# Xattn and mixture-of-experts layer on one core: the first stage with loads in order of use, a query projection in two halves, and large GpSimd work put later

## The reference

```python
x = x + xattn(layernorm(x), ctx)      # x (8, 112, 512), ctx (8, 375, 128)
x = x + ffn(layernorm(x))

def xattn(q, latent_kv):              # 16 heads of 32
    qp = q @ Wq.T                     # (512, 512)
    k, v = split(latent_kv @ Wkv_expand.T, 2)
    scores = einsum('bhqd,bhkd->bhqk', qh, kh) / sqrt(32)
    attn = softmax(where(tril, scores, min))
    return (attn @ vh) @ Wout.T

def ffn(h):                           # 896 tokens, 8 experts, the best 2 of each token
    combine = top2(softmax(h @ gate.T))
    y = sum_e combine[e] * (silu(h @ gate_e.T) * (h @ up_e.T)) @ down_e.T
    return y + shared_expert(h)
```

## Time and profile before

| | |
|---|---|
| median of 3 runs | 365.05 us (364.71 to 365.6) |
| profiled execution | 365.72 us |
| its span, first to last instruction | 364.0 us |
| mean granted TensorE clock | 0.985 |
| busy, share of the span | PE 94%, PEld 77%, DVE 70%, ACT 64%, POOL 28% |
| instructions | 6,824 |

### The profile page before, as it was taken

One profiled execution on the slowest core, in us unless ns is written; L12 is line 12 of the kernel. 1 busy time (PEld: TensorE's weight loads), 2 busy tenths in 40 slices (PEclk: granted clock), 3 DMA queues, 4 the chain that ended last, 5 costly groups with the idle time before them and its releaser, 6 DMA issues.

```text
span 364.0 us, 6824 instructions
## 1 busy us (share of the span) xinstructions
PE 340.8 (94%) x2212; PEld 280.3 (77%) x2213; DVE 255.8 (70%) x460; ACT 231.5 (64%) x607; POOL 101.3 (28%) x111
## 2 busy tenths in 40 slices
PE   5599899999999998999999899999999999999992
PEld 5487778677777676898898788878888887888871
DVE  2994885899975518782676897787778778777810
ACT  3525888999976222512136488888887887888731
POOL 3649221455550000054600003112211311221131
PEclk9889999999999999999999999999999999999997
DMA  7999000000000859995779753543444354344333
GB/s 226 366 367 377 27 2 2 3 2 0 3 3 2 307 167 398 357 392 193 257 245 216 262 163 58 81 90 60 66 82 84 58 82 92 59 67 82 53 38 52
DMA packets 28458, 49.46 MB, mean 136 GB/s; under 512 B 6672, under 2 KB 11792, under 8 KB 27408
## 3 DMA queue, kind: packets, MB, share of 16 engines
q1 hardware_dynamic: 24288, 39.91, 33.6%
q0 software_dynamic: 4144, 9.23, 14.8%
HBM read 32.22 MB, written 16.92 MB: 135 GB/s over the span
## 4 chain that ended last, share of the span: by engine, by line
PE 71%; ACT 13%; DMA 6%; DVE 5%; issue 3%; POOLq 1%; POOL 0%; SPq 0%; DVEq 0%; ACTq 0%
PE bank L501 30%; PE bank L778 21%; ACT prob L900 9%; PE bank L793 9%; DMA out<-y_sb,dest 3%; PE bank L684 3%; PE bank L817 2%; DMA w_kv<-wkvT 2%; PE bank L656 2%; PE bank L493 1%; ACT probT L855 1%; DMA w_sg<-sguT 1%; DVE xn L1122 1%; PE bank L670 1%; PE bank L579 1%
## 5 line engine op out<-in xcount | busy, mean ns | idle before, releaser
L1129 DVE TENSOR_TENSOR gu_parts<-w_gu,gu_parts 128x704 fp32r<-128x704 f32 x84 | 72.8, 888 | 21.2 <-ACT gu_parts L855 19.7
L855 ACT ACTIVATE gu_parts<-w_gu 128x704 fp32r x84 | 66.1, 790 | 15.8 <-PE bank L778 15.4
L482 POOL DMA_INDIRECT out<-y_sb,dest x21 | 33.1, 1575 | 145.7 <-ACT y_sb L1050 137.7
L778 PE MATMUL bank<-gu_parts,xsT_hi 128*128 128x352 f32 x336 | 69.9, 330 | 1.2 <-issue 1.2
L778 PEld LDWEIGHTS bank<-gu_parts,xsT_hi 128*128 128x128 f32 x336 | 55.3, 189 | 2.2 <-issue 2.2
L778 PE MATMUL bank<-gu_parts,xsT_lo 128*128 128x352 f32 x168 | 40.8, 324 | 0.0
L793 PE MATMUL bank<-w_dn,actT_plain 128*128 (+1 forms) x80 | 37.7, 592 | 0.0
L501 PE MATMUL bank<-x2T_hi,w_sg_lo 128*128 128x512 f32 (+1 forms) x88 | 32.2, 365 | 0.1
L501 PE MATMUL bank<-x2T_hi,w_sg_hi 128*128 128x512 f32 (+1 forms) x88 | 31.9, 363 | 0.0
L501 PE MATMUL bank<-x2T_lo,w_sg_hi 128*128 128x512 f32 (+1 forms) x88 | 31.9, 363 | 0.0
L778 PEld LDWEIGHTS bank<-gu_parts,xsT_lo 128*128 128x128 f32 x168 | 29.3, 189 | 0.0
(11 more groups left out here) (199 smaller groups left out, 769.9 us busy)
## 6 DMA issues: line engine op xcount, KB each, us to landing
w_gu<-guT SPq DMA_DIRECT2D x8, 1408.0 KB
xs_dram<-xs_in SPq DMA_DIRECT2D x1, 5460.0 KB, 20.3
xs_in<-xs_dram SPq DMA_DIRECT2D x21, 256.0 KB, 2.7
w_dn<-dnT SPq DMA_DIRECT2D x8, 512.0 KB, 5.2
w_sg<-sguT SPq DMA_DIRECT2D x10, 256.0 KB
xres<-x SPq DMA_DIRECT2D x2, 768.0 KB, 9.6
w_dn<-dnT SPq DMA_DIRECT2D x8, 192.0 KB, 5.5
w_sd<-sdnT SPq DMA_DIRECT2D x5, 256.0 KB, 6.1
```

Source lines behind the costliest of these rows:

```text
L482: pool.indirect_dma_start(out=out[:, :], out_offset=bass.IndirectOffsetOnAxis(ap=dest[:, i, 0:1], axis=0), in_=y_sb[i % 2][:, :], in_offse ...
L778: ins = pe.matmul(dst[:, 0:F], xsT[x_][:, c, :], gu2[w_][:, c, f0:f0 + F], start=c == 0 and n == 0, stop=c == C - 1 and n == 2)
L855: act.activation(dst, src, ACT.Copy).then_inc(s[sem], 1)
L1129: dve.tensor_tensor(lo_, src, hi_.bitcast(F32), ALU.subtract).then_inc(s[sem], 1)
```

## The change

The loads are issued in another order and in smaller pieces: x tile 0, ctx 0, the key half of w_kv, x tile 1, x tiles 2 and 3, w_q in four chunks of 128 rows, the value half of w_kv, the remaining x tiles, ctx 1, w_o, then the shared weights. The keys are made before `t1(1)`. The query projection of the first four tiles is made in two halves: first 256 tokens (tiles 0 and 1) chunk by chunk, each chunk waiting only for its own split, with the transposes of tiles 2 and 3 between; then the other 256 tokens, block j by block j, with the transposes of tiles 4 to 6 behind blocks 1 to 3. GpSimd's subtractions of w_kv and w_q go to VectorE. GpSimd splits w_o in eight pieces after the seventh normalised tile, and fills the constants after attention block 1. The split of the first slices of the shared weights goes to attention block 1, on ScalarE before `put_oT(1)` and on VectorE before `oT_lo(1)`. In the diff below, the list of semaphore names and the body of the constants, which moved unchanged, are cut.

```diff
--- before.py
+++ after.py
@@ -227,11 +227,11 @@
...
@@ -258,13 +258,17 @@
                 at = slice(k * BLK, (k + 1) * BLK)
                 sp.dma_start(ctx[:, at, :], ctxT[:, at, 0:SQ]).then_inc(s[f"ctx{k}"], 16)
+            sp.dma_start(xres[:, 0, :], x_rows[0:P, :]).then_inc(s["x0"], 16)
             load_ctx(0)
-            sp.dma_start(xres[:, 0, :], x_rows[0:P, :]).then_inc(s["x0"], 16)
-            sp.dma_start(w_kv[:, :], wkvT).then_inc(s["wkv"], 16)
-            sp.dma_start(xres[:, 1:BLK, :], tiles_of(x_rows, 1, BLK)).then_inc(s["x0b"], 16)
-            sp.dma_start(w_q[:, :, :], wqT.rearrange("(c p) d -> p c d", p=P)).then_inc(s["wq"], 16)
+            sp.dma_start(w_kv[:, 0:H], wkvT[:, 0:H]).then_inc(s["wkeys"], 16)
+            sp.dma_start(xres[:, 1, :], x_rows[P:2 * P, :]).then_inc(s["xt1"], 16)
+            sp.dma_start(xres[:, 2:BLK, :], tiles_of(x_rows, 2, BLK)).then_inc(s["xt2"], 16)
+            for c in range(C):
+                sp.dma_start(w_q[:, c, :], wqT[c * P:(c + 1) * P, :]).then_inc(s[f"wq{c}"], 16)
+            sp.dma_start(w_kv[:, H:2 * H], wkvT[:, H:2 * H]).then_inc(s["wvals"], 16)
             sp.dma_start(xres[:, BLK:NX, :], tiles_of(x_rows, BLK, NX)).then_inc(s["xrest"], 16)
             load_ctx(1)
+            sp.dma_start(w_o[:, :, :], woT.rearrange("(c p) d -> p c d", p=P)).then_inc(s["wo"], 16)
             def load_sg(j):
@@ -280,7 +284,6 @@
             load_sg(0)
             load_sd(0)
-            sp.dma_start(w_o[:, :, :], woT.rearrange("(c p) d -> p c d", p=P)).then_inc(s["wo"], 16)
             sp.dma_start(w_gate[:, :, :], gateT).then_inc(s["wgate"], 16)
             load_sg(1)
             load_sd(1)
@@ -406,41 +409,35 @@
             rstd(0, "st1", var1, rstd1, mv1, "rs1a", "rs1b")
-            pool.wait_ge(s["wkv_hi"], 1)
-            pool.tensor_tensor(w_kv2[1][:, H:2 * H], w_kv[:, H:2 * H], w_kv2[0][:, H:2 * H].bitcast(F32), ALU.subtract)\
-                .then_inc(s["wkv_lo2"], 1)
-            for n in range(1, BLK):
+            for n in range(1, NX):
                 rstd(n, "st1", var1, rstd1, mv1, "rs1a", "rs1b")
-            pool.wait_ge(s["wq_hi"], 1)
-            half = slice(C // 2, C)
-            pool.tensor_tensor(w_q2[1][:, half, :], w_q[:, half, :], w_q2[0][:, half, :].bitcast(F32), ALU.subtract)\
-                .then_inc(s["wq_lo2"], 1)
-            for n in range(BLK, NX):
-                rstd(n, "st1", var1, rstd1, mv1, "rs1a", "rs1b")
+            pool.wait_ge(s["xn"], NX)
             pool.wait_ge(s["wo"], 16)
-            pool.tensor_copy(w_o2[0][:, :, :], w_o[:, :, :]).then_inc(s["wo_hi"], 1)
-            pool.wait_ge(s["wo_hi"], 1)
-            pool.tensor_tensor(w_o2[1][:, :, :], w_o[:, :, :], w_o2[0][:, :, :].bitcast(F32), ALU.subtract)\
-                .then_inc(s["wo_lo"], 1)
-            own(pool.memset(tri[:, :], 1.0))
...
-            pool.iota(token, [[P, NX], [0, 1]], base=0, channel_multiplier=1).then_inc(s["tok"], 1)
+            for c in range(C):
+                pool.tensor_copy(w_o2[0][:, c, :], w_o[:, c, :]).then_inc(s["wo_hi"], 1)
+            for c in range(C):
+                pool.wait_ge(s["wo_hi"], c + 1)
+                pool.tensor_tensor(w_o2[1][:, c, :], w_o[:, c, :], w_o2[0][:, c, :].bitcast(F32), ALU.subtract)\
+                    .then_inc(s["wo_lo"], 1)
+            def constants():
+                own(pool.memset(tri[:, :], 1.0))
...
+                pool.iota(token, [[P, NX], [0, 1]], base=0, channel_multiplier=1).then_inc(s["tok"], 1)
             def apply2(n):
                 pool.wait_ge(s["rs2b"], n + 1)
                 pool.tensor_scalar(x2n[:, n, 0:H], xres[:, n, :], mv2[:, n, 0:1], rstd2[:, n, :],
@@ -452,6 +449,8 @@
                     apply2(n - 3)
                 for r in range(RP, R):
                     normalised(n, r)
+                if n == 1:
+                    constants()
             for n in (NX - 2, NX - 1):
                 rstd(n, "st2", var2, rstd2, mv2, "rs2a", "rs2b")
@@ -513,6 +512,11 @@
             def q_proj(k, j, bank_):
                 product(bank_[:, 0:WX[k]], [(both(w_q2, every, c, slice(j * P, (j + 1) * P)), both(xnT[k], every, c, every))
                                         for c in range(C)]).then_inc(s["Q"], 1)
+            def q_part(c, j, cols, bank_):
+                return product(bank_[:, cols], [(both(w_q2, every, c, slice(j * P, (j + 1) * P)), both(xnT[0], every, c, cols))],
+                               start=c == 0, stop=c == C - 1)
             def k_proj(k, j, bank_):
                 product(bank_[:, 0:W], [(both(w_kv2, every, slice(j * P, (j + 1) * P)),
@@ -583,20 +587,34 @@
             t1(0, S[0])
             for what in ("ctx_hi", "ctx_lo", "wkv_hi", "wkv_lo"):
                 pe.wait_ge(s[what], 1)
-            k_proj(0, 0, bank[4])
-            for j in range(1, C):
+            for j in range(C):
                 k_proj(0, j, bank[4 + j])
-                t1(j, S[j])
-            pe.wait_ge(s["xnT_lo"], 2)
-            keep_busy(S[0:2], 5)
-            for what, value in (("wq_hi", 2), ("wq_lo", 1), ("wq_lo2", 1), ("xnT_hi", BLK), ("xnT_lo", BLK)):
-                pe.wait_ge(s[what], value)
+            t1(1, S[1])
+            keep_busy(S[2:4], 6)
+            first, second = slice(0, 2 * P), slice(2 * P, 4 * P)
+            for c in range(C):
+                pe.wait_ge(s["wq_hi"], c + 1)
+                pe.wait_ge(s["wq_lo"], c + 1)
+                if c == 0:
+                    pe.wait_ge(s["xnT_hi"], 2)
+                    pe.wait_ge(s["xnT_lo"], 2)
+                for j in range(C):
+                    if c == 0:
+                        pe.wait_ge(s["KT"], j + 1)
+                    q_part(c, j, first, bank[4 + j])
+                if c in (1, 2):
+                    t1(c + 1, S[c + 1])
+            pe.wait_ge(s["xnT_hi"], BLK)
+            pe.wait_ge(s["xnT_lo"], BLK)
             for j in range(C):
-                pe.wait_ge(s["KT"], j + 1)
-                q_proj(0, j, bank[4 + j])
-                if BLK + j < NX:
-                    t1(BLK + j, S[j])
-            pe.wait_ge(s["wkv_lo2"], 1)
+                for c in range(C):
+                    ins = q_part(c, j, second, bank[4 + j])
+                ins.then_inc(s["Q"], 1)
+                if j >= 1:
+                    t1(BLK + j - 1, S[j - 1])
+            pe.wait_ge(s["wkv_hi"], 2)
+            pe.wait_ge(s["wkv_lo"], 2)
             pe.wait_ge(s["QT"], C - 1)
             v_proj(0)
             pe.wait_ge(s["xnT_hi"], NX)
@@ -637,8 +655,8 @@
                         if b >= 3:
                             pe.wait_ge(s["x1"], b - 2)
                         if b == 2:
-                            pe.wait_ge(s["wo_hi"], 1)
-                            pe.wait_ge(s["wo_lo"], 1)
+                            pe.wait_ge(s["wo_hi"], C)
+                            pe.wait_ge(s["wo_lo"], C)
                         out_proj(b - 2, 0, 7)
                     if r == 1 and b >= 3:
                         t2(b - 3, CC)
@@ -917,26 +935,32 @@
                 hi(ctx2[0][:, at, :], ctx[:, at, :], "ctx_hi")
             ctx_hi(0)
-            act.wait_ge(s["wkv"], 16)
-            hi(w_kv2[0][:, :], w_kv[:, :], "wkv_hi")
+            def wkv_hi(sem, at):
+                act.wait_ge(s[sem], 16)
+                hi(w_kv2[0][:, at], w_kv[:, at], "wkv_hi")
+            def wq_hi(c):
+                act.wait_ge(s[f"wq{c}"], 16)
+                hi(w_q2[0][:, c, :], w_q[:, c, :], "wq_hi")
+            wkv_hi("wkeys", slice(0, H))
             put_xnT(0, S[0])
             put_kT(0, 0, bank[4])
-            act.wait_ge(s["wq"], 16)
-            for j in range(1, C):
-                if j <= 2:
-                    at = slice((2 - j) * C // 2, (3 - j) * C // 2)
-                    hi(w_q2[0][:, at, :], w_q[:, at, :], "wq_hi")
-                put_kT(0, j, bank[4 + j])
-                put_xnT(j, S[j])
+            put_kT(0, 1, bank[5])
+            wq_hi(0)
+            put_kT(0, 2, bank[6])
+            put_xnT(1, S[1])
+            put_kT(0, 3, bank[7])
+            for c in range(1, C):
+                wq_hi(c)
+            put_xnT(2, S[2])
+            wkv_hi("wvals", slice(H, 2 * H))
+            put_xnT(3, S[3])
             ctx_hi(1)
             for j in range(C):
                 put_qT(0, j, bank[4 + j])
-                if BLK + j < NX:
-                    put_xnT(BLK + j, S[j])
-                if j == 1:
-                    sg_hi(0)
-                if j == 2:
-                    sd_hi(0)
+                if j >= 1:
+                    put_xnT(BLK + j - 1, S[j - 1])
             put_v(0)
             for r in range(R):
                 exps(0, r)
@@ -963,6 +987,8 @@
                     exps(b + 1, 1)
                 if b == 1:
                     put_qT(1, 3, D)
+                    sg_hi(0)
+                    sd_hi(0)
                 if b == NB - 1:
                     sg_hi(1)
                     sd_hi(1)
@@ -1212,39 +1238,47 @@
```

(83 more changed lines are left out.)

20 lines of the change are left out of this document (16 added, 4 removed).

## The result

The changed kernel took 359.32 us (median, 359.11 to 360.0) against 364.88 for the kernel before beside it: ratio 0.9843, 95% interval 0.9822 to 0.9865, so 5.56 us or 1.6% faster. The forecast was 360.0, with a gain of 5.06. The profiled execution took 359.25 us with a span of 357.5; its mean granted clock is 0.996.

The account below looks back on a forecast made before the run. The wait chain bounds the start: weight landing, stopped VectorE steps, then TensorE's projection; ScalarE sets attention. 6.75 − 1.69 = 5.06 us off the profiled 365.72 gives 360.66, so 360.0 for the median; range 357.6 to 363.6.

Parts of the forecast that it names:

- Keys: First stage: keys land at 6.15, two splits follow, K starts near 7.6 us instead of 11.07.
- Projection: Query projection in halves: starts at 12.65, 96 matmuls 0.12 us apart, last product out at 26.45.
- low-clock rival: Projection at 1.2 GHz: for part, +2.3 us, 362.3, chance 0.12; or throughout, +9.2 us, 369.2, chance 0.08.
- Landings: Loads at 377 KB/us: x tile 1 at 7.96 us, w_q chunks at 10.0, 10.7, 11.4 and 12.0.
- Transfers in series: Rival on the loads: each begins when the previous has landed, 2.2 us each; 362.8 us, chance 0.06.
- The exposed end: Last tile's chain between last product and scores, now exposed: 1.85 us, with scores at 28.3.
- GpSimd: Split of w_o ends near 31.6, hidden by 2 us before VectorE's first probability product at 33.6.
- The rival's mechanism: Block 0: GpSimd's w_o pieces hold VectorE steps, one piece costing 1.2 us; 361.2 us, chance 0.04.
- The moved splits: Shared-weight splits on ScalarE's unbroken chain in block 1: 1.69 us lost, between 1.5 and 2.0.
- The sum: Whole kernel: 6.75 us gained at the scores minus 1.69 for the moved splits, 5.06 us.

Follow-up runs that it names:

- second profile: Profile of a repeat measurement of the changed kernel with no edit; 360.66 us, ratio 0.9871 to the kernel before.
- wo_whole: Changed kernel with GpSimd splitting w_o in two whole steps, without waiting for the seventh normalisation; 360.44 us, ratio 0.9866 to the kernel before.
- split_gap: Changed kernel with the shared-weight splits moved, within block 1, to where ScalarE and VectorE idled; 358.98 us, ratio 0.9821 to the kernel before.
- one_pass: Changed kernel with the query projection in one pass of 512 tokens, waiting for all chunks and tiles; 366.36 us, ratio 1.003 to the kernel before.
- split_back: Changed kernel with the shared-weight splits back beside the projection and before VectorE's first maxima; 361.73 us, ratio 0.9877 to the kernel before.
- pool_sub: Changed kernel with the subtractions of w_q and w_kv given back to GpSimd; 361.17 us, ratio 0.9902 to the kernel before.
- back_no_read: split_back with GpSimd's four w_o subtractions replaced by zero fills that read nothing; 358.74 us, ratio 0.9815 to the kernel before.
- no_fill: Changed kernel without the filler transposes, 24 before the keys and 12 before the projection; 361.68 us, ratio 0.9899 to the kernel before.

## Why the prediction was right, step by step

The forecast held. From the projection on it held by the mechanism that it gave; the start of the keys came right by luck.

**Keys.** K was put at 7.6, from a landing at 6.15 and two splits, and came at 7.54, on another path. The keys were there sooner, as ScalarE's timeline shows (after):

```profile
5.37 0.63 ACT L873 ACTIVATE w_kv_hi<-w_kv 128x512 fp32r<-128x512 f32 x1 [0.37 <-DMA w_kv<-wkvT]
```

By the prediction's own costs K would have followed near 6.8. But tile 0 was not ready: its transposes stand ahead of K in TensorE's queue, and its normalisation ahead of the keys' low part in VectorE's. The chain of the second profile runs over GpSimd's `rstd` of that tile:

```profile
4.85 1.10 POOL rstd L408
...
5.97 0.56 DVE xn L1148
...
6.57 0.66 PE bank L492 x4
...
7.26 2.66 PE bank L500 x12
```

In the first profile the 24 fillers end at 6.83, just then, and stand on the chain instead. The prediction left tile 0 out of its sum for K and put the landing 0.8 us too late; the two cancel. Its path does show in wo_whole and split_gap, where the keys were there later and K waited for them, until 8.17 and 7.62.

**Projection.** It was put at 12.65 and came at 12.36; its last product out at 26.45 and 26.11. The 12 fillers took 1.64 us of the chain and not 1.1, and ended last, not VectorE's work. The 256-column matmuls ran 0.12 apart with the clock at 1.00, so neither low-clock rival came about here. one_pass shows that the danger was real: there TensorE idled, the low clock appeared and the gain was gone.

**Landings.** Tile 1 was there by 7.30 (statistics on VectorE) instead of 7.96, chunk 0 by 9.49 instead of 10.0. The rate of 377 KB/us, 386 GB/s, was a little low: the windows from 6 to 11 us show 391 to 408. Transfers in series, at 2.2 us each, would have brought chunk 0, the sixth, at about 13; they are excluded.

**The exposed end** was sized well: 1.85 us taken, 1.95 measured, from 26.11 to 28.06. The transposes of tile 6 cost nothing, since they end at 26.55, while ScalarE still copies Q; its copy of tile 6 follows without a wait:

```profile
26.65 0.59 ACT L873 ACTIVATE xnT_hi<-bank 128x512 fp32r<-128x512 f32 x1
```

The scores came at 28.06, not 28.3: 6.99 us gained instead of 6.75.

**GpSimd.** The split of w_o ended at 32.00 instead of 31.6. The cover was 1.3 us and not 2. split_back shows what lies behind it: two VectorE steps 1.33 us longer in sum, and in the profiled execution a clock that falls. The rival's mechanism is thus right, and in that kernel its price of 1.2 us too low. For the step that reads a bank and one SBUF tile the prediction named a row of 13.16, which had no large GpSimd step beside it. pool_sub has such a pair, and there the step isn't stopped: 0.68 us from 17.36 on, beside a GpSimd subtraction from 17.11 to 18.59.

**The moved splits** were put at 1.69, with 1.5 as the lower bound. split_gap measures 1.45 to 1.49: neighbouring copies overlap by some 0.15 us each, as the prediction had allowed for.

**The sum.** 6.99 − 1.53 = 5.46 us at the end of the attention, against 5.06 predicted, and 5.56 in the medians. The second profile gained 5.70 at that point and its medians 4.71, so the forecast lies between the two measurements. The profiled execution gained 6.47; the other 1.0 lies in the third stage, in the main in a wait of 3.73 us for w_sg, where the chain of the kernel before has

```profile
130.71 4.64 DMA w_sg<-sguT
```

The second profile of the same code, with 245.09 for the rest, does not have this gain.

**What carried the gain.** Undone alone, each part lets the scores slip: the halves by 5.80 us, the loads by 3.06 (one transfer for w_q alone by 1.05), the subtractions on VectorE by 1.66. They add up to more than the 6.99 gained, as parts do that only pay together; that reading is argued, since no run takes out two of them. The prediction summed times along one path and didn't ask which part was needed for which.

## What to carry to other kernels

Cut a product along what arrives first when you reorder the loads: while the first instruction still waited for the last of them, in one_pass, the projection started 3.36 us earlier, and with the low clock behind it only 1.19 us of that reached the scores. Add up every path into an instruction, the short ones too: the one through tile 0 set the start of the keys and was in no sum. Place work that is put off into a gap of its engine that the timeline shows, not just "later" (1.45 us here), and look at what reads SBUF on GpSimd at that time before giving VectorE a two-input step. Compare profiles of single executions at a point up to which two runs of the same code agree.

## What the runs showed of the hardware that was not expected

- Between the profiles of back_no_read and split_back, a delay of 1.33 us on VectorE became 4.20 at `put_oT(1)`. TensorE's idle time grew from 1.15 to 2.42 us in between, and its granted clock was 0.50 for the next 6 us. How much of the 4.20 the clock alone costs isn't shown.
- In the first microseconds the column of the granted clock isn't borne out by the pace: in no_fill it prints 1.00 from 8 to 9 us, while 448 columns took 0.37 us, the pace that the earlier trace rows shows at the low level (0.36).
- The 24 fillers into one bank ran 0.27 us apart; 12 into two banks took 0.15 each (1.80 us from 10.52, after). That one bank makes them serial is only argued. TensorE's timeline shows no idle time there, and the clock fell nevertheless, to 0.50 from 39 to 45 us. The 24 transposes into four banks ahead of the keys went with the higher pace of K; without them, in no_fill, it was the lower one.
- The stop works both ways: GpSimd's four pieces took 6.42 us beside VectorE's steps and 5.00 without.
